# Window attention and Fourier mixing on one core: two variances computed as four small products, one of them fed by a transfer, in another order of stages

## The chip, the cores and the metric

The kernel runs on one core of a Trainium2 chip. Its five engines (TensorE, VectorE, ScalarE, GpSimd and SyncE; in the rows PE with PEld for its weight loads, DVE, ACT, POOL and SP) run each its own list of instructions in order and meet at semaphores. The metric is device microseconds of one launch, lower is better. All arithmetic is in 32-bit floats.

## What is computed

The input `x` is 8 x 256 x 256 x 64. Layer 0 is a window attention block with two norms, layer 1 a filter along the first image axis:

```python
a = shifted_window_attention(x, ...)          # windows of 4 x 4 pixels, 4 heads of 16 channels
x = x + layernorm(a, norm1_g, norm1_b)        # over the 64 channels of a pixel
h = gelu(x @ fc1_w.T + fc1_b) @ fc2_w.T + fc2_b   # 64 -> 256 -> 64
x = x + layernorm(h, norm2_g, norm2_b)
# layer 1: moving average + rfft -> 128 modes x (w_real + i w_imag) -> irfft
x = trend + irfft(einsum('bmnc,cmk->bknc', rfft(x - trend)[:, :128], W))
```

Both norms subtract the mean by their weights (the second factor of the projection and of fc2 has its mean taken off beforehand), so what is left of a norm at run time is a variance: the squares of 64 channels are averaged, `v = mean(d * d)`, and `d / sqrt(v + eps)` is formed as `d * exp(-0.5 * ln(v + eps))`.

## The kernel before

The kernel has three parts in time: a short one that makes the mixing matrices of layer 1 (lines 385 to 411 on TensorE), the long one of layer 0, and the last one that applies the mixing matrices channel by channel (lines 545 to 560).

The long part walks over 512 groups of 32 x 16 pixels in each half of the image width. A tile has 128 partitions: 64 channels of the left half (a = 0) above 64 channels of the right half (a = 1). Each engine runs the same software pipeline: `step` calls, in an order written out by hand, one function for each stage, each for another group; `i0` is the newest group, `i1` the one before it, and so on to `i7`. Sixteen steps are written out as straight code, then a loop runs over the rest (one step in each pass on TensorE, four on ScalarE and VectorE, eight on GpSimd), then seven steps drain it. `need` puts a wait for a stage of a group ahead of an instruction, `after` does so for the last user of a shared buffer, `settled` puts a semaphore instruction ahead of a batch of matmuls that takes up the waits.

TensorE's order of a step (lines 527 to 540) is: turn x (L424), first half of the weighted values pvA (L475), first hidden half fc1a (L511), pvB (L475), fc2a and fc2b (L523), projection (L487), first half of q, k, v, qkvA (L436), variance 2 (L501), variance 1 (L495), qkvB (L436), scores (L453), fc1b (L511). A matmul of 32-bit floats is two instructions, each with a weight load. Several stages cut the 128 x 128 array into tiles with `tile_position`, so that products of distinct tiles can run side by side: fc1 and qkv use tiles of 64 rows, fc2 and the projection tiles of 64 columns, scores and weighted values 32 x 32. The two variances use the whole array: `ones` is 128 x 128 with 1/64 in its two diagonal blocks of 64 x 64 and zero elsewhere.

PSUM has eight banks of 512 columns. Before the change: M (banks 0, 1) is used in turn by qkv and fc1; S (bank 2) by the scores; PV (the first halves of banks 3 and 4) by the weighted values, with variance 2 in bank 3; D1 (bank 5) by the projection and the turned x; H2 (bank 6) by fc2; TR (bank 7) by variance 1.

ScalarE's order (lines 666 to 681): load of the table with exp and ln (L666), softmax exponent (L617), ln of variance 1 (L635), ln of the q, k norms (L604), root 1 (L641), ln of variance 2 (L652), root of the q, k norms (L611), root 2 (L658), load of the gelu table (L674), gelu 1 (L664), keep x (L592), squares of q, k (L599), keep o (L623), gelu 0 (L664), squares 2 (L647), squares 1 (L630). Gelu 1 is that of the hidden half that TensorE computed last in its step before.

SyncE issues the eight transfers of a group of x as soon as the x before it is turned (`load_x`, L315 to L319), and every fourth group the store of a finished stripe (`store_y`).

## Time and profile before

| | |
|---|---|
| time, median of 3 runs | 8854.63 us (8853.43 to 8855.93) |
| the profiled execution | 8850.95 us, span 8849.2 us |
| mean granted TensorE clock | 0.967 |
| PE busy | 8401.3 us (95% of the span) |
| ACT busy | 6230.1 us (70%) |
| DVE busy | 5742.6 us (65%) |
| POOL busy | 5155.6 us (58%) |
| transfers | 700 MB, mean 79 GB/s |

Busy time is the union of an engine's instructions; a busy TensorE need not run at its peak. The page also cuts the span into 40 slices. In the first two slices the mixing matrices are made, from the third on the groups run evenly up to slice 34, and in the last six slices the transfers of layer 1 take over (DMA engines 60 to 90% busy, TensorE 80%).

### The profile page before, as it was taken

The numbers are of one execution on the slowest core, as the hardware profiler recorded it, in microseconds if no ns is written. First come the engines' busy times: TensorE is split into PE (matmuls) and PEld (weight loads), VectorE is DVE, ScalarE is ACT, GpSimd is POOL, SyncE is SP. The second block draws the span as 40 slices with busy tenths as digits, with TensorE's granted clock in tenths as the row PEclk, the third lists the DMA queues.
The fourth block names the chain that finished last, engine by engine and source line by source line (L and its number), as shares of the span: only waits on it lengthen the run. The fifth ranks groups of instructions, "written<-read, shape, count | busy, mean of one in ns | idle before, by whom it ended". The sixth has DMA issues, their size and how long they took to land.

```text
span 8849.2 us, 652880 instructions
## 1 busy us (share of the span) xinstructions
PE 8401.3 (95%) x291636; PEld 5471.0 (62%) x291636; DVE 5742.6 (65%) x8029; ACT 6230.1 (70%) x8530; POOL 5155.6 (58%) x5127
## 2 busy tenths in 40 slices
PE   8799999999999999999999999999999999878686
PEld 5556666666666666666666666666666666557565
DVE  1457777777777777777777777777777777222121
ACT  1468888888888888888888888888888888322121
POOL 0357777777777777777777777777777777100000
PEclk9789999999999999999999999999999999889888
DMA  3111111111111111111111111111111111699999
GB/s 99 39 32 38 37 38 38 38 38 37 38 38 38 38 38 37 38 37 35 36 38 37 38 38 38 38 37 38 38 38 38 37 37 36 202 324 319 337 317 332
DMA packets 1105192, 700.01 MB, mean 79 GB/s; under 512 B 616850, under 2 KB 1026834, under 8 KB 1100948
## 3 DMA queue, kind: packets, MB, share of 16 engines
q1 hardware_dynamic: 1100484, 564.33, 23.9%
q10 hardware_dynamic: 4608, 134.22, 3.5%
q8 instruction: 80, 1.31, 0.1%
q14 instruction: 20, 0.16, 0.0%
HBM read 412.97 MB, written 285.21 MB: 79 GB/s over the span
## 4 chain that ended last, share of the span: by engine, by line
PE 93%; DMA 4%; issue 1%; SPq 0%; POOL 0%; DVE 0%; ACTq 0%; ACT 0%; POOLq 0%; DVEq 0%
PE ps L475 15%; PE ps L453 13%; PE ps L511 12%; PE ps L523 11%; PE ps L436 10%; PE ps L551 10%; PE ps L501 6%; PE ps L487 5%; PE ps L495 5%; PE ps L424 3%; DMA out<-arena 3%; PE ps L398 1%; PE ps L389 1%; PE ps L390 1%; SPq L262 0%
## 5 line engine op out<-in xcount | busy, mean ns | idle before, releaser
L475 PEld LDWEIGHTS ps<-arena 32*32 32x32 f32 x131072 | 1290.9, 104 | 541.8 <-issue 508.4
L475 PE MATMUL ps<-arena 32*32 32x16 f32 x131072 | 1425.4, 186 | 17.9 <-issue 12.6
L664 ACT ACTIVATE arena<-ps,arena 128x1024 f32<-128x1024 f32 x1024 | 1140.4, 1114 | 357.8 <-PE ps L523 205.9
L775 DVE TENSOR_TENSOR arena<-ps,arena 128x768 f32<-128x768 f32 x1024 | 962.1, 940 | 539.3 <-PE ps L436 539.3
L913 POOL TENSOR_TENSOR arena<-arena 128x512 f32<-128x512 f32 x512 | 536.9, 1049 | 1282.9 <-DVE arena L846 1009.9
L453 PEld LDWEIGHTS ps<-arena 32*32 32x32 f32 x131072 | 1167.1, 105 | 152.6 <-issue 152.6
L453 PE MATMUL ps<-arena 32*32 32x16 f32 x131072 | 1218.9, 180 | 34.3 <-issue 34.3
L960 POOL TENSOR_TENSOR arena<-arena 128x512 f32<-128x512 f32 x512 | 629.5, 1230 | 1037.6 <-DVE arena L827 1037.6
L551 PE MATMUL ps<-xch,amat 128*128 128x256 f32 x4096 | 924.6, 388 | 288.0 <-ACT arena L688 214.3
L511 PE MATMUL ps<-arena 64*128 64x512 f32 x4096 | 1178.9, 652 | 8.6 <-ACT arena L664 4.5
L922 POOL TENSOR_TENSOR arena<-arena 128x512 f32<-128x512 f32 x1024 | 1044.0, 1041 | 10.5 <-PE ps L475 10.4
L551 PEld LDWEIGHTS ps<-xch,amat 128*128 128x128 f32 x4096 | 784.8, 194 | 428.3 <-ACT arena L688 219.2
L523 PE MATMUL ps<-arena 128*64 128x512 f32 x4096 | 1016.8, 617 | 1.8 <-DVE arena L852 1.4
L436 PEld LDWEIGHTS ps<-arena 64*128 64x128 f32 x8192 | 646.7, 187 | 596.5 <-issue 486.0
L436 PE MATMUL ps<-arena 64*128 64x192 f32 x8192 | 950.6, 351 | 9.9 <-DVE arena L775 7.2
L801 DVE STREAM_TRANSPOSE arena<-arena 128x1024 f32<-128x1024 f32 x512 | 638.2, 1246 | 487.7 <-POOL arena L945 487.7
L688 ACT ACTIVATE arena<-ps 128x512 f32 x256 | 270.9, 1065 | 938.4 <-PE ps L551 612.0
L881 DVE COPY arena<-ps 128x512 f32 x256 | 268.0, 1052 | 943.0 <-PE ps L551 628.7
L592 ACT ACTIVATE arena<-ps 128x512 f32<-128x512 f32 x512 | 305.9, 598 | 577.2 <-POOL arena L913 542.8
L977 POOL TENSOR_TENSOR ystripe<-arena 128x512 f32<-128x512 f32 x512 | 654.6, 1278 | 41.6 <-DVE arena L858 41.6
L674 ACT ACT_TABLE_LOAD x519 | 665.9, 1283 | 9.1
L666 ACT ACT_TABLE_LOAD x519 | 665.9, 1283 | 9.1
(89 smaller groups left out, 14021.8 us busy)
## 6 DMA issues: line engine op xcount, KB each, us to landing
arena<-in_x SPq DMA_DIRECT2D x4096, 32.0 KB
y<-ystripe SPq DMA_DIRECT2D x256, 512.0 KB, 5.3
amat<-mix SPq DMA_DIRECT2D x512, 256.0 KB, 3.4
xch<-y SPq DMA_DIRECT2D x512, 256.0 KB, 4.0
out<-arena ACTq DMA_DIRECT2D x32, 4096.0 KB, 27.1
mix<-amat SPq DMA_DIRECT2D x64, 256.0 KB, 2.0
wri<-in_w_real SPq DMA_DIRECT2D x64, 64.0 KB, 1.8
wri<-in_w_imag SPq DMA_DIRECT2D x64, 64.0 KB, 1.9
```

Of the source, the lines that this page charges most:

```text
L436: ins = mm(M[:, a, pl * 256:pl * 256 + 3 * C], xT[a * C:a * C + C, 2 * pp + pl, :], wqkv[a * C:a * C + C, :], start=True, stop=True, tile_ ...
L453: ins = mm(S[r, c0 + e:c0 + 32:2], qT[r, sl, q, e:64:2], kT[r, sl, q, e:32:2], start=True, stop=True, tile_position=(32 * cg, 32 * cg))
L475: ins = mm(PV[32 * h:32 * h + 32, b, c0:c0 + N], vexp[r, sl, h, :, :], pT[r, sl, h // 2, h % 2, :], start=True, stop=True, tile_position=( ...
L511: ins = mm(M[:, a, :], w1[a * C:a * C + C, kk * P:(kk + 1) * P], x1T[a * C:a * C + C, :], start=True, stop=True, tile_position=(a * C, 0))
L523: ins = mm(H2[a * C:a * C + C, :], w2[:, kk, :], hT[kk][:, a, :], start=(kk == 0), stop=(kk == 1), tile_position=(0, a * C))
L551: ins = mm(ps[:, j, k * T:(k + 1) * T], amat[j][:, r * T + k * P:r * T + (k + 1) * P], xch[j][:, r * T:(r + 1) * T], start=(r == 0), stop= ...
L664: f(hT[kk], M, ACT.Gelu, bias=b1[:, kk:kk + 1]).then_inc(done, 1)
L666: act.preload_act_table_set(EXP_SET)
L674: act.preload_act_table_set(GELU_SET)
L775: tt(qkv[ring(g, 4)][:, :, 4 * pp:4 * pp + 4, :].rearrange("p w s n -> p s w n"), M.rearrange("p a (s n) -> p (a s) n", s=2)[:, :, 0:3 * C ...
L922: tt(vexp.rearrange("p s h e d -> p (s h) e d")[:, :, e, :], qkv[ring(g, 4)][:, 2].rearrange("p s (h d) -> p (s h) d", h=HEADS), par[:, e: ...
L977: tt(ystripe[r // GPS][:, :, r % GPS, :].rearrange("p r (n j) -> p n r j", j=WIN), yg.rearrange(v, r=ROWS, j=WIN), x1o[ring(g, 4)].rearran ...
```

## The change

It touches layer 0 alone.

- The two variances of a step become one stage, `variances(i5, i7)`, at the start of TensorE's step. Each is two products of 64 x 64 tiles instead of one of 128 x 128. Variance 2 takes the two diagonal tiles of the array, variance 1 the two others, so the four products have four distinct tiles. A tile off the diagonal reads one half of the partitions and writes the other, so the squares of the first norm are copied with their halves swapped (`sq1x`) by two transfers of 128 KB that SyncE issues behind the x loads (`swap_halves`).
- The banks: PV moves to 5 and 6, D1 to 3, H2 to 4; variance 1 shares bank 6 with PV, variance 2 has bank 7 alone; the turned x shares bank 2 with the scores.
- Another order of stages on TensorE, ScalarE, VectorE and GpSimd. On TensorE the second half of qkv moves to the next step, pvA and pvB stand next to each other, and fc2a and fc2b are parted by fc1a and the projection.

```diff
-        PV = ps[:, 3:5, 0:256]
-        D1, H2, TR = ps[:, 5, :], ps[:, 6, :], ps[:, 7, :]
-        XT, V1, V2 = D1, TR, PA
+        PV = ps[:, 5:7, 0:256]
+        D1, H2 = ps[:, 3, :], ps[:, 4, :]
+        V1, V2 = ps[:, 6, :], ps[:, 7, :]
+        XT = ps[:, 2, :]
...
+            def swap_halves(g):
+                if there(g):
+                    need(sp, sq1_sb, g)
+                    for a in range(2):
+                        sp.dma_start(sq1x[a * C:a * C + C, :], sq1[(1 - a) * C:(2 - a) * C, :]).then_inc(sq1x_in, 16)
...
                     load_x(d * 2 + k // GPS, k % GPS, Group(d * 8, k))
+                    swap_halves(Group(d * 8, k - SWAP))
...
                             need(pe, pT_sb, g)
                             need(pe, v0_sb, g)
                             need(pe, v1_sb, g)
-                            after(pe, (l2_sb, i7), (oT_sb, before(g)))
+                            after(pe, (l1_sb, i5, i7), (oT_sb, before(g)))
                         else:
                             need(pe, pvA_ps, g)
...
-                def variance1(g):
...
-                        mm(V1, ones, sq1, start=True, stop=True).then_inc(var1_ps, 1)
-
-                def variance2(g):
...
-                        mm(V2, ones, sq2, start=True, stop=True).then_inc(var2_ps, 1)
...
+                def variances(g, h):
+                    if there(g) or there(h):
+                        need(pe, sq1x_in, g, 32)
+                        need(pe, sq2_sb, h)
+                        after(pe, (oT_sb, i5), (l1_sb, before(g), before(h)))
+                        settled(pe)
+                        if there(g):
+                            for a in range(2):
+                                b = 1 - a
+                                ins = mm(V1[b * C:b * C + C, :], ones[a * C:a * C + C, a * C:a * C + C],
+                                         sq1x[a * C:a * C + C, :], start=True, stop=True, tile_position=(a * C, b * C))
+                        if there(h):
+                            for a in range(2):
+                                ins = mm(V2[a * C:a * C + C, :], ones[a * C:a * C + C, a * C:a * C + C],
+                                         sq2[a * C:a * C + C, :], start=True, stop=True, tile_position=(a * C, a * C))
+                        ins.then_inc(var_ps, 1)
...
+                variances(i5, i7)
                 turn_x(i0)
+                project_qkv(i1, 1, M, qkvB_ps)
                 weighted(i4, 0, pvA_ps)
-                first_layer(i5, 0, fc1a_ps)
                 weighted(i4, 1, pvB_ps)
                 second_layer(i6, 0, fc2a_ps)
+                first_layer(i5, 0, M, fc1a_ps)
+                project(i4)
                 second_layer(i6, 1, fc2b_ps)
-                project(i4)
-                project_qkv(i0, 0, qkvA_ps)
-                variance2(i6)
-                variance1(i4)
-                project_qkv(i0, 1, qkvB_ps)
+                first_layer(i5, 1, M, fc1b_ps)
                 scores(i2, 0)
                 scores(i2, 1)
-                first_layer(i5, 1, fc1b_ps)
+                project_qkv(i0, 0, M, qkvA_ps)
...
                 act.preload_act_table_set(EXP_SET)
-                exponent(i4)
                 log1(i5)
+                log2(i7)
                 log_norm(i2)
                 root1(i5)
-                log2(i7)
                 root_norm(i2)
                 root2(i7)
+                square(i1)
+                exponent(i3)
                 act.preload_act_table_set(GELU_SET)
-                gelu(i6, 1, fc1b_ps, fc2b_ps, gelu1)
+                keep_o(i4)
+                gelu(i5, 0, M, fc1a_ps, fc2a_ps, gelu0)
                 keep_x(i0)
-                square(i1)
-                keep_o(i4)
-                gelu(i5, 0, fc1a_ps, fc2a_ps, gelu0)
+                square1(i4)
+                gelu(i5, 1, M, fc1b_ps, fc2b_ps, gelu1)
                 square2(i6)
-                square1(i4)
...
-                turn_q(i2)
-                sum_squares(i1)
-                turn_k(i2)
                 clamp(i1)
-                qkv_out(i0, 0, qkvA_ps, qkvA_sb)
-                sum_prob(i3)
-                invert(i3)
-                qkv_out(i0, 1, qkvB_ps, qkvB_sb)
+                bias(i2)
+                qkv_out(i0, 0, M, qkvA_ps, qkvA_sb)
+                turn_prob(i3)
+                maximum(i2)
+                qkv_out(i0, 1, M, qkvB_ps, qkvB_sb)
                 normed1(i4)
-                turn_prob(i3)
                 normed2(i6)
                 add1(i4)
-                bias(i2)
-                maximum(i2)
                 gain2(i6)
+                turn_q(i1)
+                sum_prob(i2)
+                invert(i2)
+                turn_k(i1)
+                sum_squares(i0)
...
+                divide(i3)
                 add_o2(i5)
-                expand_v(i3)
-                divide(i3)
-                norm_k(i1)
-                add_o1(i0)
+                shift(i2)
                 scale_norm(i1)
                 norm_q(i1)
+                add_o1(i0)
+                norm_k(i1)
+                expand_v(i2)
                 add2(i6)
-                shift(i2)
```

## Rows read from the trace of the kernel before

**Rows 1.** Page, part 4: shares of the chain of work that ended last.

```profile
PE 93%; DMA 4%; issue 1%; SPq 0%; POOL 0%; DVE 0%; ACTq 0%; ACT 0%; POOLq 0%; DVEq 0%
```

**Rows 2.** Windows: us, busy us of each engine, granted clock, DMA share, GB/s.

```profile
560.00:3000.00 2440.00, 2436.39 (x97172) 1527.43 (x97171) 1840.22 (x2604) 1999.76 (x2777) 1749.45 (x1738) 1.00 0.17 37
7400.00:7480.00 80.00, 80.00 (x3156) 49.99 (x3144) 61.09 (x86) 66.52 (x94) 58.05 (x58) 1.00 0.14 32
```

**Rows 3.** Timeline of PE, one step: start us, us, engine, line, operation.

```profile
4011.53 0.66 PE L424 MATMUL ps<-arena 128*128 128x128 f32 x4
4012.11 1.39 PE L475 MATMUL ps<-arena 32*32 32x16 f32 x128
4013.43 1.13 PE L511 MATMUL ps<-arena 64*128 64x512 f32 x4
4014.49 1.42 PE L475 MATMUL ps<-arena 32*32 32x16 f32 x128
4015.84 1.94 PE L523 MATMUL ps<-arena 128*64 128x512 f32 x8
4017.61 1.03 PE L487 MATMUL ps<-arena 128*64 128x256 f32 x8
4018.58 0.92 PE L436 MATMUL ps<-arena 64*128 64x192 f32 x8
4019.43 1.13 PE L501 MATMUL ps<-arena 128*128 128x512 f32 x2
4020.39 1.02 PE L495 MATMUL ps<-arena 128*128 128x512 f32 x2
4021.34 0.92 PE L436 MATMUL ps<-arena 64*128 64x192 f32 x8
4022.19 2.33 PE L453 MATMUL ps<-arena 32*32 32x16 f32 x256
4024.45 1.13 PE L511 MATMUL ps<-arena 64*128 64x512 f32 x4
4025.51 0.66 PE L424 MATMUL ps<-arena 128*128 128x128 f32 x4
```

**Rows 4.** Instructions of L243 on PE's sequencer: ns min/median/max, first and last start.

```profile
L243 PEldq COMPARE_BRANCH  x7: 207/208/208, 4010.4 to 4094.4; - x7
```

**Rows 5.** Timeline of PE in a warm-up step with pvA and pvB adjacent.

```profile
316.39 1.28 PE L475 MATMUL ps<-arena 32*32 32x16 f32 x101 [0.44 <-issue]
318.00 0.42 PE L475 MATMUL ps<-arena 32*32 32x16 f32 x27 [0.33 <-PE ps L475]
```

**Rows 6.** Timeline of ACT, its run of short operations in a step.

```profile
4014.37 1.05 ACT L599 ACTIVATE arena<-arena 128x1024 f32<-128x1024 f32 x1
...
4021.45 0.69 ACT L635 ACTIVATE arena<-ps,arena 128x512 f32<-128x512 f32 x1
4022.03 0.25 ACT L604 ACTIVATE arena<-arena 128x64 f32<-128x64 f32 x1
4022.18 0.62 ACT L641 ACTIVATE arena<-arena 128x512 f32<-128x512 f32 x1
4022.70 0.67 ACT L652 ACTIVATE arena<-ps,arena 128x512 f32<-128x512 f32 x1
4023.27 0.34 ACT L611 ACTIVATE arena<-arena 128x64 f32<-128x64 f32 x1
4023.51 0.62 ACT L658 ACTIVATE arena<-arena 128x512 f32<-128x512 f32 x1
4024.15 1.28 ACT L674 ACT_TABLE_LOAD   x1
```

**Rows 7.** Timeline of SP: the eight issues of one group's x.

```profile
4012.35 5.60 SPq L319 DMA_DIRECT2D arena<-in_x  x8
```

**Rows 8.** Page, part 6: KB of each issue, us from issue to landing.

```profile
xch<-y SPq DMA_DIRECT2D x512, 256.0 KB, 4.0
...
mix<-amat SPq DMA_DIRECT2D x64, 256.0 KB, 2.0
```

## What the change does to the time

> **What bounds the kernel now.** I read the chain that ended last first: 93% of the span is TensorE [rows 1]. Then the windows of the long part: from 560 to 7480 us TensorE is busy all the time at a granted clock of 1.00, which is the 2.4 GHz level, while ScalarE is busy 82% (1999.76 of 2440 us), VectorE 75% and GpSimd 72% [rows 2]. Then one step on TensorE [rows 3]: from one turn of x to the next 13.98 us, every group of matmuls starting where the one before it stops. 6920 / 13.98 gives 495 such steps, and a microsecond more or less in the step is 495 us. The other engines have room but not much: 82% of 13.98 is 11.5 us for ScalarE.
>
> The parts of the step, start to start [rows 3]: turn 0.58, pvA 1.32, fc1a 1.06, pvB 1.35, fc2 1.77, projection 0.97, qkvA 0.85, variances 0.96 + 0.95, qkvB 0.85, scores 2.26, fc1b 1.06.
>
> **Four small products for two large ones.** 1.91 us go. The nearest row for what comes is fc1: two products of 64-row tiles and 512 columns, four matmul instructions, 1.06 us, about what one whole-array product (0.95) takes, so distinct tiles do run side by side [rows 3]. Four tiles of 64 x 64 are one step further than any row; if all four overlap, 1.06: **-0.85**. Ends: 1.0, and 1.91 if nothing is won.
>
> What supports four at once while variance 1 sends both halves of its result into one bank: the scores do the same in small. Their 256 matmuls go from all four row strips into bank 2 and take 2.26 us, 8.8 ns each; a whole-array matmul instruction streams 512 columns in 0.48 us, so 16 columns take 15 ns, and more than one must be in flight in that bank [rows 3]. The Trainium skill (TensorEngine Tiling (Array Packing), Restrictions and Gotchas) says that different row tiles cannot access the same PSUM bank simultaneously. By that rule variance 1's two products take turns, and the stage stays near 1.9 us; the row of the scores speaks against it where the partitions are disjoint, as they are here.
>
> **pvA and pvB next to each other.** pvB waits for pvA's semaphore. Before, fc1a lay between them and hid it; now TensorE stands. The one place where the trace has them adjacent is a warm-up step: pvB starts 0.33 us after pvA's end [rows 5]. In the loop pvA ends, by its row, 1.39 us after its start, 0.07 later than fc1a starts [rows 3]. The whole 0.33 makes it 0.33 + 0.07 = 0.40 dearer, nothing makes it 0. That step is without matmuls queued ahead, so I take a little over the middle: **+0.22**.
>
> **fc2a and fc2b parted.** fc2 and the projection run now as one batch of column tiles. fc2a alone needs an entry and an exit of its own: a pair of fc1 products costs 1.06 where half of fc2 costs 1.77 / 2 = 0.89, so about 0.17 for one pair of changes of tile shape [rows 3]: **+0.16**, ends 0 and 0.2. The Trainium skill (same page, Tiling Modes) says that changing the tiling mode drains TensorE. The list of stages has ten changes of shape before and ten after, so by that rule alone this term would be 0 and the step 0.16 shorter.
>
> **pvA behind both logarithms.** Variance 1 shares bank 6 with PV, so pvA now waits for log1 and, by the way the wait is written, for log2 too. From the start V of the variances: their last product ends at V + 1.13 (fc1's duration), log1 starts 0.04 later as L635 does behind L495, log2 0.58 after it, and lasts 0.67: V + 2.42 [rows 3, 6]. TensorE reaches pvA at 1.06 + 0.58 + 0.85 = V + 2.49. With a reaction of up to the 0.33 us of rows 5 that is a stall of 0 to 0.3: **+0.14**. Everything TensorE has to do stands behind it.
>
> **The loop's turn.** The branch takes 0.21 us on the sequencer [rows 4] and four waits of the variances follow it. Now they lie under fc1b (1.06), then under qkvA (0.85), right behind the scores, where no queue is built up. 0 to 0.3: **+0.10**.
>
> Sum: 13.98 - 0.85 + 0.22 + 0.16 + 0.14 + 0.10 = **13.75 us**. The turn, both qkv, the scores, fc1 and the projection keep their cost; the eight small matmul instructions for four large ones are paid in the 1.06.
>
> **What else could be late in a step of 13.75.** *ScalarE.* log1 at V + 1.17, then start to start as in rows 6: 0.58, 0.57 (log2), 0.15, 0.52, 0.24, 0.52, squares of q, k 1.05, exponent 0.64, table 1.28: keep_o starts at 6.72 and, as long as L658, ends at V + 7.34. TensorE reaches the projection at 1.06 + 0.58 + 0.85 + 0.14 + 2.67 + 0.22 + 1.05 + 1.06 = 7.63. Margin 0.29, the smallest of all. *The swap.* Behind the projection and fc1a, ScalarE does gelu 0, keep_x and squares 1, in all some 1.05 + 0.62 + 0.69, from V + 7.7 to 10.1. SyncE has issued the eight x loads by then (turn ends at 1.7, they take 5.6 us [rows 7]), reacts in some 0.2, issues two transfers 0.7 apart (5.6 / 8) and the second lands 2.0 us later, as the store of an SBUF tile to HBM does [rows 8]: V + 13.0. Needed at 13.75, less what the waits take, about 13.4. Margin 0.4. Behind SyncE's new wait are only the next x loads, which wait for a later turn anyway, and the y store. *VectorE and GpSimd* have the same work as before, 10.5 and 10.0 us in a step [rows 2], and each of their new orders starts from a result that TensorE or ScalarE gives half a step earlier than it is needed; only qkvB's copy (0.9 us) lies close ahead of the squares of q, k.
>
> So the steps go from 13.98 to 13.75: 0.23 x 495 = 114 us off the profiled 8851 us, 8737; the median stands 3.7 us above the profiled run: **8741 us**. The warm-up, the drain and layer 1 are left as they are, within 10 us.
>
> **Rivals.**
>
> *The new stalls are cheap (8600).* The reactions in a running loop are short, so that half of the 0.62 us of new costs is not there: step 13.44, 0.54 x 495 = 267 less. For it: TensorE's groups now follow one another within 0.1 us. Against: each of those had its data long before.
>
> *ScalarE's ring sets the pace (8860).* Variances, logarithms, roots, squares, exponent, table, keep_o, projection, back to the variances is one ring. If its instructions wait each for the one before (durations instead of starts: 0.69, 0.67, 0.25, 0.62, 0.34, 0.62, 1.05, 0.63, 1.28, 0.62 = 6.77), oT is ready at V + 7.94, and with a reaction of 0.1 TensorE goes on at 8.04 instead of 7.63: step 14.0 to 14.2, time 8860 to 8960, no gain. For it: the margin is 0.29 us and the chain is long. Against: rows 6 show starts closer than durations.
>
> *The four products take turns (slower, 9160).* One mechanism: TensorE doesn't run two row halves into one bank, or not four tiles at once. Then the stage costs 1.91 instead of 1.06 while all new costs stay: step 14.60, 0.62 x 495 = 307 more than now. It decides from the point where less than 0.62 of the 0.85 us is won. This is also the case in which the change doesn't do what it says.
>
> *The swap lands late (slower, about 9200).* The variances stand at the head of the step, and everything waits behind them. A transfer of 4.0 us (the loads of layer 1 under traffic [rows 8]) would make V + 15.0 and a step of over 15; 3.5 us gives 14.66, 9190. It costs from a landing of 2.4 us on and makes the kernel slower than now from 2.8. Against: in this part the DMA engines are busy 17% [rows 2].
>
> **Chances.** The forecast's case 0.49 (8650 to 8830), cheap stalls 0.18, ScalarE's ring 0.13, turns 0.11, late swap 0.09. A measurement of this kernel can tell about 0.2%, 18 us. Faster: 0.49 + 0.18 + 0.02 of the ring's case = 0.69. Same: 0.06 of the ring's case and 0.02 of the swap's: 0.08. Slower: the rest, 0.23. The range leaves out the half of the cheap case that goes to its end and most of the two slow ones: **8560 to 8960**.
>
> **What would show it.** In a timeline of TensorE: the variances as one group of eight matmuls of 64 x 64 within some 1.1 us (1.9: turns); a gap of 0.2 to 0.3 us ahead of pvB; a stall of 0.1 to 0.2 ahead of pvA, put down to ScalarE; a period of 13.75. In the waits: TensorE's idle time ahead of the projection means ScalarE's ring, ahead of the variances with a DMA named means the swap. SyncE should wait for the squares and not for its own issues. The prediction is wrong if the step isn't between 13.4 and 13.95.

## The result and the profile after

The changed kernel takes 10171.03 us (10144.49 to 10237.22), the kernel before on the same chip 8855.28 us (8853.43 to 8860.99): ratio 1.1496, 95% interval 1.1441 to 1.1551. It is 1316 us slower where 114 us less were forecast.

The windows of the changed kernel: length, busy us of PE, PEld, DVE, ACT, POOL with the number of instructions, granted clock, DMA share, GB/s.

```profile
560.00:1000.00 440.00, 411.99 (x15035) 240.81 (x15023) 273.55 (x397) 298.49 (x424) 268.32 (x267) 0.87 0.22 49
...
3000.00:5000.00 2000.00, 1935.42 (x68068) 1108.16 (x68056) 1253.04 (x1810) 1362.05 (x1932) 1209.25 (x1204) 0.83 0.21 48
...
7400.00:8700.00 1300.00, 1257.39 (x43442) 714.84 (x43440) 801.62 (x1157) 871.89 (x1234) 776.66 (x774) 0.81 0.21 46
```

Two things differ from [rows 2]: TensorE is no longer busy all the time, 1935 of 2000 us, and its granted clock, 1.00 before, is 0.81 to 0.87. VectorE does 15 instructions in a step, so 1810 of them are 120.7 steps: 16.57 us a step, where 13.98 stood [rows 3]. This count gives all the mean steps below.

One step on TensorE, to be laid beside [rows 3]: start, us, engine, line, operation, and the idle time ahead with what ended it.

```profile
4001.84 0.65 PE L525 MATMUL ps<-arena 64*64 64x512 f32 x2
4001.85 0.65 PE L529 MATMUL ps<-arena 64*64 64x512 f32 x2
4002.32 0.60 PE L525 MATMUL ps<-arena 64*64 64x512 f32 x2
4002.33 0.60 PE L529 MATMUL ps<-arena 64*64 64x512 f32 x2
4002.86 0.66 PE L449 MATMUL ps<-arena 128*128 128x128 f32 x4
4003.45 0.92 PE L461 MATMUL ps<-arena 64*128 64x192 f32 x8
4004.51 1.43 PE L500 MATMUL ps<-arena 32*32 32x16 f32 x128
4006.36 1.60 PE L500 MATMUL ps<-arena 32*32 32x16 f32 x128 [0.41 <-PE ps L500]
4007.89 1.98 PE L553 MATMUL ps<-arena 128*64 128x512 f32 x4
4009.80 2.08 PE L541 MATMUL ps<-arena 64*128 64x512 f32 x4
4011.80 1.93 PE L512 MATMUL ps<-arena 128*64 128x256 f32 x8
4013.56 1.03 PE L553 MATMUL ps<-arena 128*64 128x512 f32 x4
4014.52 1.13 PE L541 MATMUL ps<-arena 64*128 64x512 f32 x4
4015.58 2.39 PE L478 MATMUL ps<-arena 32*32 32x16 f32 x256
4017.90 0.92 PE L461 MATMUL ps<-arena 64*128 64x192 f32 x8
4018.75 0.65 PE L525 MATMUL ps<-arena 64*64 64x512 f32 x2
```

The four small products start within 10 ns of each other and take 1.02 us (4001.84 to 4002.86): that part works. Then fc2a takes 1.91, fc1a 2.00 and the projection 1.76, start to start, where fc1a has 1.06 and the projection 0.97 in [rows 3]: about twice as long. The granted clock of the same step says why (same columns as the windows above, the granted clock third from the end):

```profile
4006.00:4006.50 0.50, 0.14 (x29) 0.17 (x33) 0.50 (x2) 0.50 (x1) 0.50 (x1) 1.00 0.16 33
4006.50:4007.00 0.50, 0.50 (x71) 0.50 (x64) 0.50 (x2) 0.50 (x2) 0.23 (x1) 0.73 0.29 65
4007.00:4007.50 0.50, 0.50 (x68) 0.50 (x58) 0.50 (x2) 0.48 (x2) 0.01 (x1) 0.50 0.17 38
...
4013.00:4013.50 0.50, 0.50 (x4) 0.24 (x2) 0.00 (x0) 0.50 (x2) 0.50 (x1) 0.50 0.00 0
4013.50:4014.00 0.50, 0.50 (x5) 0.14 (x2) 0.00 (x0) 0.16 (x2) 0.50 (x1) 0.94 0.00 0
```

From about 4006.7 to 4013.6, 6.8 us of the 16.9, TensorE has its lower level, 1.2 GHz. It costs some 0.9 each for fc2a, fc1a and the projection, 2.7 us, so that without it the step would be 14.2. A few steps do keep the upper level with both waits in them. One of them as a window, and its rows around pvB:

```profile
4196.82:4211.10 14.28, 13.70 (x566) 8.49 (x564) 11.21 (x15) 11.20 (x16) 10.04 (x10) 1.00 0.36 83
```

```profile
4201.35 1.54 PE L500 MATMUL ps<-arena 32*32 32x16 f32 x128 [0.41 <-PE ps L500]
4202.86 1.08 PE L553 MATMUL ps<-arena 128*64 128x512 f32 x4
...
4205.84 1.03 PE L553 MATMUL ps<-arena 128*64 128x512 f32 x4
```

That step takes 14.28 us, where 13.98 stood: the new order is no gain even at a granted clock of 1.00. Of 37 steps between 3800 and 4400 us, 21 have the low level in all three operations, 10 in a part of them and 6 in none.

The view of the waits from 3000 to 5000 us gives the rest: SyncE waits 4.7 us in each step (567.2 us in 120 times) for the squares that it has to swap, and no idle time of TensorE ahead of the variances or the projection is put down to a DMA or to ScalarE.

### The profile page after: what moved, and what is told of

It is laid out like the page before. It is cut to its first block, busy times and chain, and to the rows that moved or that the text cites. A ratio compares the mean times of both kernels' runs of the same rounds, so it can differ in the third digit from the quotient of the medians.

```text
span 10166.0 us, 659875 instructions
## 1 busy us (share of the span) xinstructions
PE 9406.2 (93%) x293684; PEld 5667.5 (56%) x293684; DVE 5631.7 (55%) x8029; ACT 6113.5 (60%) x8530; POOL 5146.5 (51%) x5127
## 4 chain that ended last, share of the span: by engine, by line
PE 93%; DMA 3%; issue 3%; SPq 0%; ACT 0%; ACTq 0%; DVE 0%; POOL 0%; POOLq 0%; DVEq 0%
PE ps L500 16%; PE ps L541 15%; PE ps L553 13%; PE ps L478 12%; PE ps L461 9%; PE ps L512 8%; PE ps L580 8%; PE ps L525 5%; PE ps L449 3%; DMA out<-arena 3%; PE ps L423 1%; PE ps L414 1%; PE ps L415 1%; SPq L277 0%; DMA xch<-y 0%
## 5 line engine op out<-in xcount | busy, mean ns | idle before, releaser
L983 POOL TENSOR_TENSOR arena<-arena 128x512 f32<-128x512 f32 x512 | 625.7, 1222 | 2961.9 <-DVE arena L843 2961.9
L835 DVE TENSOR_TENSOR arena<-ps,arena 128x512 f32<-128x512 f32 x512 | 354.2, 692 | 2929.8 <-PE ps L478 2929.8
L500 PE MATMUL ps<-arena 32*32 32x16 f32 x131072 | 1535.3, 192 | 320.0 <-PE ps L500 195.5
L500 PEld LDWEIGHTS ps<-arena 32*32 32x32 f32 x131072 | 1422.3, 110 | 532.5 <-issue 495.7
L541 PE MATMUL ps<-arena 64*128 64x512 f32 x4096 | 1580.6, 858 | 0.0
L553 PE MATMUL ps<-arena 128*64 128x512 f32 x4096 | 1485.3, 812 | 5.8 <-DVE arena L881 5.8
L478 PEld LDWEIGHTS ps<-arena 32*32 32x32 f32 x131072 | 1199.8, 105 | 448.4 <-issue 432.5
L478 PE MATMUL ps<-arena 32*32 32x16 f32 x131072 | 1266.9, 180 | 43.3 <-issue 33.7
L951 POOL TENSOR_TENSOR arena<-arena 128x512 f32<-128x512 f32 x1024 | 1041.1, 1036 | 30.2 <-PE ps L500 30.1
L541 PEld LDWEIGHTS ps<-arena 64*128 64x128 f32 x4096 | 402.3, 240 | 1173.0 <-issue 1086.7
L942 POOL TENSOR_TENSOR arena<-arena 128x512 f32<-128x512 f32 x512 | 597.2, 1166 | 660.1 <-DVE arena L875 388.4
L512 PE MATMUL ps<-arena 128*64 128x256 f32 x4096 | 902.6, 587 | 0.7 <-ACT arena L652 0.7
L512 PEld LDWEIGHTS ps<-arena 128*64 128x64 f32 x4096 | 363.5, 201 | 887.9 <-issue 857.5
L910 DVE COPY arena<-ps 128x512 f32 x256 | 267.9, 1052 | 945.7 <-PE ps L580 630.4
L664 ACT ACTIVATE arena<-ps,arena 128x512 f32<-128x512 f32 x512 | 352.3, 688 | 729.2 <-PE ps L529 716.8
L461 PEld LDWEIGHTS ps<-arena 64*128 64x128 f32 x8192 | 655.0, 189 | 112.0 <-issue 90.1
```

The source lines that it names most:

```text
L461: ins = mm(M[:, a, pl * 256:pl * 256 + 3 * C], xT[a * C:a * C + C, 2 * pp + pl, :], wqkv[a * C:a * C + C, :], start=True, stop=True, tile_ ...
L478: ins = mm(S(sl)[r, c0 + e:c0 + 32:2], qT[r, sl, q, e:64:2], kT[r, sl, q, e:32:2], start=True, stop=True, tile_position=(32 * cg, 32 * cg))
L500: ins = mm(PV[32 * h:32 * h + 32, b, c0:c0 + N], vexp[r, sl, h, :, :], pT[r, sl, h // 2, h % 2, :], start=True, stop=True, tile_position=( ...
L512: ins = mm(d1[a * C:a * C + C, :, e, :], wpe[:, e, :], oT[:, a, :, :], start=True, stop=True, tile_position=(0, a * C))
L541: ins = mm(M[:, a, :], w1[a * C:a * C + C, kk * P:(kk + 1) * P], x1T[a * C:a * C + C, :], start=True, stop=True, tile_position=(a * C, 0))
L553: ins = mm(H2[a * C:a * C + C, :], w2[:, kk, :], hT[kk][:, a, :], start=(kk == 0), stop=(kk == 1), tile_position=(0, a * C))
```

## Experiments

The names are a_ for a variant of the changed kernel and b_ for one of the kernel before. Theory 1 to begin with: the clock falls because TensorE idles between pvA and pvB. Theory 2: because two halves of 32x32 products stand next to each other. Theory 3: because of the small tiles of the variances, which load the array less.

Idle time is told in two ways. What a row has in brackets counts from the end that the row gives. From start to start the same wait looks longer, since a batch that needn't wait starts 0.07 to 0.17 us before the end that the row of the one ahead gives (fc1a lasts 1.13 us and pvB follows after 1.06, fc2 1.94 and 1.77 [rows 3]): the 0.41 us ahead of pvB are 1.85 - 1.32 = 0.53 from start to start. Waits too short to have a bracket are given from start to start, and named so.

### Which of the change's parts brings the clock down

**a_no_gap**: pvB writes into other banks and no longer waits for pvA (half of the weighted values is thus left out of what follows; one product ahead of the loop, which fills bank 6 once, isn't shown).

```diff
-                            need(pe, pvA_ps, g)
+                            need(pe, qkvB_sb, i1)
                         settled(pe)
+                        dst = PV if d == 0 else M
```

> The changed kernel, with pvB written into the banks of M (free once qkvB is copied) instead of PV, so that it no longer waits for pvA: the two batches of 32 x 32 matmuls stay adjacent, the 0.4 us of idle TensorE between them go. What pvB computes is not read, so half of the weighted values in the output is left out. Theory 1 (the idle gap between pvA and pvB is what brings the granted clock down for 6.8 us of each step): clock 1.00 in the long part, step 16.9 - 2.9 - 0.5 = 13.5 us, about 8620 us. Theory 2 (two batches of 32 x 32 matmuls in a row bring it down, gap or not) and theory 3 (the small variances do): the low stretch stays, step about 16.4, about 9920 us.

Measured 9119.02 us, ratio 1.0293 (1.0235 to 1.0352), clock 0.96, 14.44 us a step. Taking away a gap of 0.41 us gave back 1052 us, 2.1 us a step. Theory 1 had 8620, the others 9920: the gap is a cause, but some steps have the low level without it. In a step at the full level the row of pvA and pvB is one batch, and fc2a stands at 1.01:

```profile
4017.20 2.96 PE L502 MATMUL ps<-arena 32*32 32x16 f32 x256
4020.18 1.08 PE L555 MATMUL ps<-arena 128*64 128x512 f32 x4
4021.19 1.13 PE L543 MATMUL ps<-arena 64*128 64x512 f32 x4
```

**b_adjacent**: the kernel before, pvB moved up.

```diff
+                weighted(i4, 1, pvB_ps)
                 first_layer(i5, 0, fc1a_ps)
-                weighted(i4, 1, pvB_ps)
```

> The kernel before, with fc1a moved behind pvB: pvA and pvB adjacent, with the wait between them, and whole-array variances as before. Theories 1 and 2: a stretch at the low clock appears in each step, 13.98 + 0.5 + about 3 = 17.4 us, about 10550 us. Theory 3: clock stays 1.00, step 14.5, about 9100 us.

Measured 9300.05 us, ratio 1.0497 (1.0467 to 1.0528), clock 0.96, 14.81 us a step, without any part of the variances' change. That too lies between the two values expected. In 14 of 40 steps between 3800 and 4400 us fc2 takes up to twice its time, in the others it doesn't:

```profile
4013.98 1.26 PE L475 MATMUL ps<-arena 32*32 32x16 f32 x128
4015.54 1.41 PE L475 MATMUL ps<-arena 32*32 32x16 f32 x128 [0.30 <-PE ps L475]
4016.88 1.13 PE L511 MATMUL ps<-arena 64*128 64x512 f32 x4
4017.94 3.60 PE L523 MATMUL ps<-arena 128*64 128x512 f32 x8
...
4033.91 1.94 PE L523 MATMUL ps<-arena 128*64 128x512 f32 x8
```

**a_whole_var**: the variances as two whole-array products (the halves of variance 1 stand exchanged).

```diff
-                            for a in range(2):
-                                b = 1 - a
-                                ins = mm(V1[b * C:b * C + C, :], ones[a * C:a * C + C, a * C:a * C + C],
-                                         sq1x[a * C:a * C + C, :], start=True, stop=True, tile_position=(a * C, b * C))
+                            ins = mm(V1, ones, sq1x, start=True, stop=True)
```

(and V2 in the same way)

> The changed kernel with the variances as two products of the whole array (variance 1 with its halves swapped, which only its values show): the same order, waits and transfers. Theories 1 and 2: the low stretch stays, step 16.9 + 0.9 = 17.8 us, about 10600 us. Theory 3 (the small tiles of the variances are what lowers the clock): 1.00, step 14.0 + 0.9 = 14.9, about 9300 us.

Measured 10123.96 us, ratio 1.1427 (1.1394 to 1.1461), clock 0.92, 16.39 us a step. **b_four_tiles**, the other way round: the kernel before with both variances as four small products in their old place, without the swap (the halves of variance 1 stand exchanged).

```diff
-                variance2(i6)
-                variance1(i4)
+                variances(i6, i4)
```

> The kernel before with the two variances as four 64 x 64 products side by side, at the place where they stood, and nothing else: no transfer swaps the halves, so variance 1 lands in the wrong half, which only its values show. Theories 1 and 2: clock 1.00, step 13.98 - 0.85 = 13.1 us, about 8430 us, if ScalarE (11.5 us busy) lets TensorE go on. Theory 3: a stretch at the low clock appears, about 9500 us or more.

Measured **8521.45 us**, ratio 0.9619 (0.9591 to 0.9647), clock 1.00, 13.25 us a step:

```profile
4020.49 0.65 PE L501 MATMUL ps<-arena 64*64 64x512 f32 x2
4020.51 0.65 PE L507 MATMUL ps<-arena 64*64 64x512 f32 x2
...
4021.51 0.92 PE L436 MATMUL ps<-arena 64*128 64x192 f32 x8
```

So the small products are worth what they promise, 13.98 - 13.25 = 0.73 us a step, and cost no clock by themselves: theory 3 falls as a cause of its own. Whole-array variances in the changed kernel raise the clock (0.92 for 0.83), but pay it back in duration, and 10124 is neither of the two values expected. That edit moves a wait as well: pvA now has 0.27 us of idle time ahead of it, put down to the second logarithm, where at most 0.15 is recorded in the changed kernel.

**a_no_gap_whole** has both edits (same parts left out), **b_adjacent_tiles** those of b_adjacent and b_four_tiles.

> The changed kernel with both edits: pvB into the banks of M (no gap, half of the weighted values left out) and whole-array variances. Each alone brought the clock from 0.83 to 0.96 and 0.92. If the clock follows how much of the array works in a step and both count: 1.00, step 13.85 + 0.9 = 14.75, about 9230 us. If it is the adjacent 32 x 32 batches themselves: still 0.96, step 15.3.

> The kernel before with pvA and pvB adjacent (clock 0.96 alone) and the four small products (clock 1.00 alone; halves swapped, only the values show it). If the two add up as in the changed kernel: clock 0.83 to 0.92, step 14.3 to 15.5, 9000 to 9600 us. If the clock takes the small products without harm: 0.96, step 14.5 - 0.8 = 13.9, about 8850 us.

Measured: 9914.52 us, ratio 1.1183, clock 0.93, 15.99 us a step; and 8738.78 us, ratio 0.9857 (0.9837 to 0.9876), clock 0.99, 13.66 us. Neither is a value expected. The effects don't add up: with the gap gone, whole-array variances lower the clock (0.93 for 0.96) and cost 795 us, with 0.27 us of idle time ahead of pvA in each step here too; and adjacent halves cost 217 us beside small products (8738.78 - 8521.45) but 440 beside whole-array ones. The gap between the halves doesn't explain that: it has the same sizes in both, 0.17 to 0.20 us in one half of the steps and 0.30 to 0.32 in the other (0.25 in the mean of both, from 3000 to 5000 us). What differs is how many steps fall: 4 of 44 have a longer fc2 beside small products, 14 of 40 beside whole-array ones. Why is open.

**a_filler**: the changed kernel with a useless whole-array product in the gap.

```diff
+                            mm(V2[:, 0:256], ones, dftm[:, 0:256], start=True, stop=True)
                             need(pe, pvA_ps, g)
```

> The changed kernel with one whole-array matmul of 256 columns, on constants and into the free bank 7, put between pvA and pvB, where TensorE stands idle for 0.4 us. It is work for nothing. If idle time alone lowers the clock: it stays near 1.00 (0.96 as in the run without the gap, or better), step some 14.4, about 9100 us, faster than the changed kernel by a tenth although it does more. If the gap is only lost time: clock 0.83 as before, 10170 us or more.

Measured 9430.22 us, ratio 1.0637 (1.0615 to 1.0658), clock 0.95, 15.04 us a step. **More work, 741 us less** (about 9100 was expected): what TensorE is doing in those 0.4 us matters more than how much there is to do. The product also parts the two halves, so this run doesn't tell a filled gap from parted halves; a_no_gap, where they stay adjacent, does.

**b_tiles_log_halves**: b_four_tiles made complete without a transfer, log1 taking the halves back in two instructions of 64 partitions.

```diff
-                        f(l1, V1, ACT.Ln, bias=eps).then_inc(l1_sb, 1)
+                        for a in range(2):
+                            b = 1 - a
+                            ins = f(l1[a * C:a * C + C, :], V1[b * C:b * C + C, :], ACT.Ln, bias=eps[b * C:b * C + C, :])
+                        ins.then_inc(l1_sb, 1)
```

> The kernel before with the four 64 x 64 products in the old place, complete this time: variance 1 lands with its halves swapped, and log1 takes them back as two instructions of 64 partitions each. No transfer. ScalarE gets 0.6 us more in the chain from the variances over log1 to gelu 1, which had 0.3 us to spare in the run with four tiles. If the gain of the four products holds without the new order: step 13.24 + 0.3 = 13.5 us, clock 1.00, about 8620 us. If the ScalarE chain takes it all back: 13.9, about 8810 us.

Measured 8997.83 us, ratio 1.015 (1.0133 to 1.0167), clock 0.98, more than either value expected. The two halves take 1.38 us together where one whole took 0.69, and ScalarE's ring sets the pace:

```profile
4013.91 1.13 PE L519 MATMUL ps<-arena 64*128 64x512 f32 x4 [0.52 <-ACT arena L674]
```

This row says one thing more: 0.52 to 0.72 us of idle time in a step, right behind pvA (0.61 in the mean), and yet a clock of 0.98. Idle time alone, with one half batch beside it, does little.

### The other wait

The gap of 0.41 us gave 2.1 us a step. But in the changed kernel TensorE idles a second time, ahead of pvA: qkvB starts at 4003.45 and lasts 0.85, pvA starts at 4004.51, so 0.21 us from start to start. The profile names no releaser for it (some steps have "[0.15 <-issue]"); log2 is the last thing pvA waits for, and runs from 4003.58 to 4004.26 in ScalarE's timeline. Four kernels ask what that is worth.

**b_gap**: the kernel before, its order kept, with pvB waiting for fc1a just ahead of it. **a_no_l2**: the changed kernel, pvA waiting for log1 alone. **a_turn_between**: the turn of x between pvA and pvB. **a_turn_no_l2**: the last two together.

```diff
 b_gap
+                            need(pe, fc1a_ps, i5)
 a_no_l2
-                            after(pe, (l1_sb, i5, i7), (oT_sb, before(g)))
+                            after(pe, (l1_sb, i5), (oT_sb, before(g)))
 a_no_l2, in the variances of the next step
+                        need(pe, l2_sb, before(h))
 a_turn_between
-                turn_x(i0)
                 project_qkv(i1, 1, M, qkvB_ps)
                 weighted(i4, 0, pvA_ps)
+                turn_x(i0)
                 weighted(i4, 1, pvB_ps)
```

> The kernel before with one wait more: the second half of the weighted values also waits for the first layer's products just ahead of it, so TensorE idles some 0.2 to 0.4 us there in each step, while the order stays as it was and the two halves are not next to each other. Nothing is left out. Theory 1 (idle time of TensorE next to the batches of 32x32 products brings the granted clock down): the clock falls below 0.99 in the long part and the time is 9100 to 9500. Theory 2 (it is the two halves standing next to each other, 256 small products in a row with little else, and not the idle time): the clock stays 1.00 and the time is 8855 plus 495 steps of 0.2 to 0.4, 8950 to 9050.

> The changed kernel, where the first half of the weighted values waits for the first norm's logarithm alone, and no longer for the second norm's (which the variances of the next step wait for). Nothing is left out. This takes away the idle 0.21 us ahead of that half and leaves the 0.41 between the halves. If every idle stretch counts for the clock: well below the changed kernel, 9600 to 10000, with the clock above 0.86. If only the gap between the halves counts: some 0.2 us a step less at most, 10050 to 10170, clock 0.83 as before.

> The changed kernel with the turn of x between the two halves of the weighted values; nothing is left out. The gap of 0.41 us between them is filled with work that has to be done anyway, but the first half, which waits for the second norm's logarithm, now comes to its wait 0.58 us earlier and idles some 0.8 us there. If the gap between the halves alone decides the clock: clock 0.98 or more, step 14.1 to 14.3, time 8900 to 9100. If idle time ahead of the halves counts as well: the clock is as low as in the changed kernel, and the time is 9700 to 10300.

> Both edits together: the turn of x between the halves, and the first half waiting for the first norm's logarithm alone. Nothing is left out. From the trace of the changed kernel that logarithm ends at 4003.68, and the products for q, k and v would end at 4003.7, so 0.2 us of idle time stay ahead of the first half and none between the halves. Step at the full clock: 1.02 + 0.85 + 0.20 + 1.35 + 0.58 + 1.35 + 1.01 + 1.06 + 0.91 + 0.96 + 1.06 + 2.40 + 0.85 = 13.60, against 13.98 before, so 8660 to 8700 where the clock stays at 1.00. If 0.2 us ahead of the first half is enough to bring the clock down in part of the steps, as 0.2 to 0.3 between the halves was in the kernel before with adjacent halves: 8850 to 9200.

Measured:

| kernel | us | ratio (95%) | clock, 3000 to 5000 us | us a step |
|---|---|---|---|---|
| b_gap | 8995.57 | 1.0151 (1.0134 to 1.0168) | 0.99 | 14.22 |
| a_no_l2 | 9073.35 | 1.0248 (1.0231 to 1.0265) | 0.95 | 14.44 |
| a_turn_between | 9390.94 | 1.0589 (1.0566 to 1.0611) | 0.94 | 14.96 |
| a_turn_no_l2 | 8881.42 | 1.0019 (1.0009 to 1.0028) | 0.98 | 14.01 |

a_no_l2 went past both expectations: 1098 us for one wait that showed 0.21 us of idle time, as much as the whole gap between the halves had given. The gap is still there, but shorter: 0.22 us in the mean for 0.39, 0.18 to 0.24 in most steps and up to 0.39 in some. In this step, as in 28 of 42, the clock stays up:

```profile
4000.21 0.92 PE L461 MATMUL ps<-arena 64*128 64x192 f32 x8
4001.06 1.41 PE L500 MATMUL ps<-arena 32*32 32x16 f32 x128
4002.67 1.43 PE L500 MATMUL ps<-arena 32*32 32x16 f32 x128 [0.19 <-PE ps L500]
4004.06 1.08 PE L554 MATMUL ps<-arena 128*64 128x512 f32 x4
```

b_gap shows that an idle stretch of 0.2 us (start to start) beside one half costs its own length and little more (14.22 - 13.98 = 0.24); its time is the one expected of theory 2. a_turn_between has 0.62 us of idle time ahead of pvA in most steps ("[0.62 <-ACT arena L681]" in its rows) but the halves apart, keeps 0.94 and lands between its two ranges. a_turn_no_l2 takes back all of the change's loss but 0.2%, in the second of its ranges. So theory 1 as it was put, any idle time next to such products, is too wide, and theory 2 alone doesn't hold either, since the halves are adjacent in the changed kernel (0.83), in a_no_gap (0.96) and in a_no_l2 (0.95).

Two kernels then ask whether this pair of idle stretches is the cause. **a_no_l2_own** puts the first one back by another wait, **b_adjacent_two** puts one into b_adjacent.

```diff
 a_no_l2_own, ahead of pvA
+                            need(pe, qkvB_ps, i1)
 b_adjacent_two, ahead of pvA
+                            need(pe, xT_ps, i0)
```

> a_no_l2 (9073 us) with a wait for TensorE's own products for q, k and v put in ahead of the first half of the weighted values. Nothing is left out. The idle time of about 0.2 us there is back, but not the wait for the second norm's logarithm. Theory 1 (the idle time is the cause): 9900 to 10200 us, clock 0.83 to 0.87, and the gap between the halves back at 0.4. Theory 2 (the logarithm's place matters in some other way): 9100 to 9250, clock 0.93.

> The kernel before with the halves of the weighted values adjacent (as in b_adjacent, 9300 us) and one more wait: the first half waits for TensorE's own turn of x, just ahead of it, so it idles some 0.2 us there too. Nothing is left out. Theory 1 (two idle stretches around the first half in one step, together with the batch of 32x32 products, are what brings the clock down in every step of the changed kernel): the clock falls to 0.80 to 0.88 and the time to 9900 to 10400. Theory 2 (the changed kernel's low clock needs something else that is its own): the added wait costs its idle time alone, 495 x 0.2 = 100 us, 9380 to 9450, clock about 0.96.

Measured: 10423.99 us, ratio 1.1768 (1.1745 to 1.1792), clock 0.80, 17.04 us a step; and 9483.58 us, ratio 1.0706 (1.0685 to 1.0728), clock 0.95, 15.20 us. A step of a_no_l2_own:

```profile
4004.70 0.92 PE L461 MATMUL ps<-arena 64*128 64x192 f32 x8
4005.88 1.41 PE L501 MATMUL ps<-arena 32*32 32x16 f32 x128 [0.27 <-PE ps L461]
4007.70 1.56 PE L501 MATMUL ps<-arena 32*32 32x16 f32 x128 [0.40 <-PE ps L501]
4009.18 1.98 PE L555 MATMUL ps<-arena 128*64 128x512 f32 x4
4011.09 2.08 PE L543 MATMUL ps<-arena 64*128 64x512 f32 x4
4013.10 1.97 PE L513 MATMUL ps<-arena 128*64 128x256 f32 x8
```

With idle time back ahead of pvA, the gap behind pvA is 0.40 again instead of 0.20, and the low level covers the same operations as in the changed kernel, in every step. So it isn't the logarithm: one wait on TensorE's own products costs 1351 us, more than theory 1 had. It is also somewhat longer than the wait it stands for, 0.33 us from start to start (4005.55 to 4005.88) where that was 0.21. In the kernel before a like wait leaves the gap at 0.17 ("[0.17 <-PE ps L476]") in every step, and 17 of 39 steps have a longer fc2, where b_adjacent had 14 of 40: nearly the second theory's value for the clock, and a time 184 us above b_adjacent, a little over its range. So the pair alone, of that size, isn't enough. The two kernels of 0.80 to 0.83 have the longest stretch in which TensorE has only 32x32 products and idle time: from the end of qkvB to the start of fc2a, 4004.30 to 4007.89 = 3.6 us in the changed kernel, 4005.55 to 4009.18 = 3.6 in a_no_l2_own. It is 3.0 in a_no_l2 (0.95) and 2.9 in b_adjacent (0.96; 4013.98 to 4016.88). But a_whole_var has 3.6 too, with the very idle times of a_no_l2_own (0.27 ahead of pvA, about 0.41 behind it), and keeps 0.92: neither the length nor the idle times alone order the runs, and what else TensorE has in the step counts.

### What keeps the best variant from 13.6

At the full level a_turn_no_l2 has steps of 13.66 us, and its scores take 2.7 to 2.9 us where 2.33 stand in [rows 3]. In its timeline the transfers of the swap are issued 0.1 to 0.4 us ahead of the scores. **a_turn_no_swap** leaves the swap out (variance 1 takes the squares in place, its halves exchanged); **a_swap_early** moves it ahead.

```diff
 a_swap_early, SyncE (six of the eight loads of x, the swap, the last two) and ScalarE
-                    load_x(d * 2 + k // GPS, k % GPS, Group(d * 8, k))
+                    load_x(d * 2 + k // GPS, k % GPS, Group(d * 8, k), range(6))
                     swap_halves(Group(d * 8, k - SWAP))
+                    load_x(d * 2 + k // GPS, k % GPS, Group(d * 8, k), range(6, 8))
...
-                keep_x(i0)
                 square1(i4)
+                keep_x(i0)
```

> a_turn_no_l2 (8881 us) without the swap: no transfers of the squares, and the first norm's variances are taken from the squares in place, so its halves stand exchanged and the output is not the reference's; every other operation is the same. If the swap's transfers, which there are issued 0.1 to 0.4 us ahead of the batch of scores, are what lengthens that batch from 2.4 to 2.7 us: the scores take 2.33 to 2.4, the step 13.3 to 13.4 at the full clock, and the time is 8500 to 8600; if the long batch also was what cost the clock, that is back at 0.99 to 1.00. If the batch is long for another reason: no change beyond 0.3%, 8860 to 8890.

> a_turn_no_l2 (8881 us) with the swap moved earlier: ScalarE takes the first norm's squares ahead of the copy of the turned x, and SyncE issues the swap after six of the eight loads of x, where it stood behind all eight, busy with them for 5.8 us up to 0.1 us before the swap. Nothing is left out. The swap then starts some 0.5 us earlier, most of it ahead of the scores. If the transfers are what lengthens the scores: scores 2.35 to 2.5 in the steps without a store of y, step 13.4 at the full clock, time 8560 to 8750. If not: 8860 to 8890.

Measured: 8729.48 us, ratio 0.9855 (0.9838 to 0.9871), clock 0.99, 13.65 us a step; and 8898.41 us, ratio 1.0048 (1.0031 to 1.0065), 13.99 us. The rows: the scores with the swap; then without it, once as a store of y goes out and once alone.

a_turn_no_l2:

```profile
3995.95 1.18 SPq L340 DMA_DIRECT2D arena<-arena  x2
3996.05 2.69 PE L478 MATMUL ps<-arena 32*32 32x16 f32 x256
```

a_turn_no_swap:

```profile
3983.30 1.50 SPq L348 DMA_DIRECT2D y<-ystripe  x2
3983.39 2.74 PE L481 MATMUL ps<-arena 32*32 32x16 f32 x256
...
4010.56 2.33 PE L481 MATMUL ps<-arena 32*32 32x16 f32 x256
```

The swap's transfers do lengthen the scores, by 0.36 us in these rows, and with them the kernel is 152 us slower. The clock wasn't saved by it as much as I expected: some steps of a_turn_no_swap still have fc2a at 1.98, so its 8729 missed the 8500 to 8600. Starting the swap 1.0 us ahead of the scores didn't help: they took 2.77 to 2.81 between 3940 and 4000 us. There the last two loads of x are issued during the scores (3960.66, the scores from 3960.32); whether they are the reason isn't shown.

## Why the prediction was wrong, step by step

**The step that failed: the clock.** The prediction read a granted clock of 1.00 in [rows 2] and took every duration from rows at that level. It priced the two new stalls as what they last: +0.22 for pvB's wait, +0.14 for pvA's. Measured, the stalls last 0.53 (pvA to pvB 1.85 instead of 1.32) and 0.21, and 2.1 us of the mean step go when either of them is removed, since together they bring 1.2 GHz for 6.8 us of most steps. The warm-up of the kernel before shows the lower level with such groups, and I read it only for a reaction time: the very step of [rows 5] ran at it. A window of that step, and a later one:

```profile
316.00:318.00 2.00, 1.28 (x102) 1.20 (x101) 1.97 (x3) 1.18 (x2) 1.23 (x1) 0.50 0.17 39
...
562.00:564.00 2.00, 2.00 (x50) 0.93 (x47) 0.97 (x3) 1.54 (x2) 1.92 (x4) 0.50 0.19 42
```

and from TensorE's timeline there:

```profile
557.97 0.76 PE L453 MATMUL ps<-arena 32*32 32x16 f32 x68 [2.21 <-issue]
...
562.46 2.08 PE L511 MATMUL ps<-arena 64*128 64x512 f32 x4
```

fc1a at 2.08 instead of 1.13 was the price list for this case; the condition for it (idle time next to 32x32 products) was one the change added. TensorE idles far more in the warm-up (2.21 us ahead of the later window, a third of the earlier one), so it would have given a rival, not a certainty.

**Four small products, -0.85:** 1.02 for 1.91, so -0.89; right. The Trainium skill (TensorEngine Tiling (Array Packing), Restrictions and Gotchas) would have them take turns in one bank; the rows say they don't. The rival "take turns" falls.

**pvA and pvB next to each other, +0.22, ends 0 and 0.40:** 0.53, beyond the upper end. The prediction took a little over the middle because the warm-up's 0.33 came from a step with nothing queued; in the loop the rows have 0.35 to 0.43 in most steps of the changed kernel and 0.19 or 0.20 in a few, mostly 0.18 to 0.24 in a_no_l2, both 0.17 to 0.20 and 0.30 to 0.32 in b_adjacent, and 0.17 throughout in b_adjacent_two, though pvA is waited for there too. Why it has two sizes stays open. Behind the gap pvB itself takes 1.51 us to the start of fc2a (4201.35 to 4202.86), 0.16 more than in [rows 3]; the prediction had nothing for that.

**fc2a and fc2b parted, +0.16:** at the full level fc2a takes 1.01 and fc2b 0.96 (4205.84 to 4206.80) for 1.77, but the projection between them 0.91 (from 4204.93) for 0.97: +0.14, right.

**pvA behind both logarithms, +0.14, ends 0 and 0.3:** 0.21 of idle time; the term was right in length, and removing it was worth 1098 us.

**The loop's turn, +0.10:** nothing; the variances start 0.85 behind qkvA, as closely as any.

**Sum at the full level:** the prediction had 13.75. With the measured terms it is 13.98 - 0.89 + 0.53 + 0.14 + 0.21 = 13.97, and with 0.16 in pvB and 0.13 in the scores (2.39 from 4207.86 to 4210.25, for 2.26), which it had at nothing, 14.26; the step measured at 1.00 takes 14.28. So two errors lie on top of one another, 0.5 us in the terms and 16.57 - 14.28 = 2.3 us of a mean step in the clock. The first alone would have made the kernel slower than before, which is not what was forecast either.

**ScalarE's ring and the late swap** didn't decide in the changed kernel: no waits of TensorE are put down to them. The ring did appear where it got 0.69 us more to do (b_tiles_log_halves), but that is the kernel before with its own order, so the margin of 0.29 us is not measured by it. The prices of the late swap don't fit together: if a landing costs from 2.4 us on, 3.5 makes a step of 14.85, not 14.66; nothing here hangs on it. In a_turn_no_l2 the swap's price was not its landing but the scores that run beside it.

The Trainium skill (TensorE: Matmul & The Clock Gate, A second HAM failure mode) describes a kernel that cycles through PSUM banks, idles briefly between groups of matmuls and whose clock goes up and down with it. This trace agrees as far as the brief idling goes, with 0.21 and 0.41 us of idle time in a step of 16.9; the prediction didn't cite it, and it would have been the rival that happened.

Open: which mix of idle time, 32x32 products and neighbours brings the level down. The runs give pairs (one edit, one clock), not the rule; a_whole_var, a_no_gap_whole and b_adjacent_two each went against the simplest one.

## What to carry to other kernels

When a change puts a wait on the engine that is always busy, don't price it by its length alone: look in the warm-up or any gap of the trace for what the same instructions cost at the lower clock, and count that as a rival. A batch of many small products was the neighbour beside which the new waits cost most here; put other work of the same engine between the producer and the wait (here the turn of x between pvA and pvB), and wait for exactly what is needed (log1, not log1 and log2). These two edits brought the changed kernel from 10171 to 8881 us, the level of the kernel before; a further 0.36 us a step (14.01 to 13.65) goes to the transfers that the exchange of halves needs.

## What the runs showed of the hardware

- A wait of TensorE on its own last matmul left 0.17 to 0.43 us of idle time between two batches of 32x32 products.
- With idle stretches of 0.21 and 0.41 us in a step around a batch of 32x32 products the granted clock went down to 0.5 for 6.8 us of most steps (0.83 in the mean); without the first it was 0.95, without the second 0.96, and one useless product of 256 columns in the second stretch brought the mean back to 0.95.
- Four 64x64 products, two and two of them into different partitions of one bank, ran at the same time: 1.02 us where two whole-array products took 1.91.
- Batches of 256 32x32 products slow down while DMAs run: 2.33 us alone, 2.69 with the swap's two transfers of 128 KB each, 2.74 with a store of y, 2.92 with both. At a granted clock of 1.00, so it isn't the clock.
- Two logarithms over 64 partitions each took 0.69 us apiece, as much as one over 128.
